# Opening stage of a two-layer perceiver kernel: load order, split of the queries, and idle products on TensorE

## What is computed

```python
x = x + _L0_xattn_ref(_layernorm(x, axis=-1), ctx_2048, ctx_2048)
# in it, with 16 heads of 16 channels, keys = values = ctx_2048:
scores = jnp.einsum('bhqd,bhkd->bhqk', qh, kh) / math.sqrt(hd)
qi = jnp.arange(Sq)[:, None] + (Sk - Sq)
ki = jnp.arange(Sk)[None, :]
causal = ki <= qi
scores = jnp.where(causal[None, None], scores, jnp.asarray(MASKED_BIAS, scores.dtype))
attn = jax.nn.softmax(scores, axis=-1)
out = jnp.einsum('bhqk,bhkd->bhqd', attn, vh)
```

## Time and profile before

| | us |
|---|---|
| three runs | 490.94, 493.5, 493.93 (median 493.5) |
| the profiled execution | 491.93, its span 490.1 |
| busy in the span: PE, DVE, ACT, POOL | 418.6, 334.4, 267.0, 110.0 |
| chain that ended last, shares | PE 63%, DVE 18%, ACT 7%, issue 6% |
| opening, up to the first product of scores | 24.94 |
| maxima of group 0, up to the copy of its maximum to rows | 24.94 to 37.91 |
| group 0 | 37.91 to 57.03 |
| group 1 | 57.03 to 73.50 |

### The profile page before, as it was taken

The page is one execution under the profiler, slowest core; times in us unless marked ns, Lnnn a source line. Parts: engine busy times, 40 slices in busy tenths (PEclk is TensorE's granted clock), DMA queues, the critical chain, the costliest instruction groups (busy, mean ns, idle before and its releaser), DMA issues.

```text
span 490.1 us, 9082 instructions
## 1 busy us (share of the span) xinstructions
PE 418.6 (85%) x3628; PEld 307.4 (63%) x3628; DVE 334.4 (68%) x537; ACT 267.0 (54%) x594; POOL 110.0 (22%) x88
## 2 busy tenths in 40 slices
PE   0168789998978898998998889996999799999997
PEld 0115556665645586486444624445889689999996
DVE  3788766678568977894366654865554788877872
ACT  4405887776758717431233315556771286777762
POOL 3002346001294010000022352233000203333300
PEclk9999999999989999999999979998899799999999
DMA  6599186543751078137200000019300595540000
GB/s 226 130 256 277 25 202 174 141 120 90 185 197 48 3 235 305 44 123 297 95 1 1 0 3 0 1 45 361 109 2 0 168 346 175 172 172 1 1 2 23
DMA packets 25002, 58.28 MB, mean 119 GB/s; under 512 B 5209, under 2 KB 13689, under 8 KB 21114
## 3 DMA queue, kind: packets, MB, share of 16 engines
q1 hardware_dynamic: 24960, 57.69, 37.2%
HBM read 44.77 MB, written 0.29 MB: 92 GB/s over the span
## 4 chain that ended last, share of the span: by engine, by line
PE 63%; DVE 18%; ACT 7%; issue 6%; POOL 2%; DMA 2%; SPq 0%; ACTq 0%; DVEq 0%; POOLq 0%
PE ps L1289 19%; PE ps L1093 9%; PE ps L924 7%; PE ps L911 5%; PE ps L880 4%; DVE mx L1666 3%; ACT reg_b L683 3%; PE ps L959 2%; PE ps L1254 2%; PE ps L1244 2%; PE ps L1243 2%; PE ps L1003 2%; POOL qreg L472 2%; PE ps L1090 1%; DMA x<-in_x 1%
## 5 line engine op out<-in xcount | busy, mean ns | idle before, releaser
L1666 DVE TENSOR_REDUCE mx<-ps 128x1 f32<-128x1024 f32 x64 | 77.0, 1221 | 36.5 <-PE ps L880 24.9
L683 ACT ACTIVATE reg_b<-ps 128x512 f32<-128x512 f32 x128 | 74.9, 598 | 26.6 <-PE ps L911 17.2
L911 PE MATMUL ps<-qreg,reg_b 98*128 98x128 bf16 x512 | 47.3, 225 | 5.7 <-ACT reg_b L683 4.2
L1093 PE MATMUL ps<-reg_b,xT 128*128 128x512 f32 x96 | 49.8, 643 | 0.0
L1289 PE MATMUL ps<-part_a 128*128 128x256 f32 x384 | 48.2, 283 | 0.4 <-DVE part_a L1819 0.4
L911 PEld LDWEIGHTS ps<-qreg,reg_b 98*128 98x128 bf16 x512 | 35.2, 100 | 19.8 <-ACT reg_b L683 9.7
L1289 PEld LDWEIGHTS ps<-part_a 128*128 128x128 f32 x384 | 46.9, 192 | 0.6 <-DVE part_a L1819 0.6
L396 POOL TENSOR_TENSOR rstd<-ve,cf 128x1 f32<-128x1 f32 x12 | 6.8, 567 | 174.0 <-DVE ve L1362 174.0
L822 ACT ACTIVATE reg_a<-ps,b 128x256 f32<-128x256 f32 x64 | 30.2, 472 | 24.4 <-PE ps L1289 24.4
L924 PE MATMUL ps<-reg_b 128*32 128x128 f32 x1024 | 43.0, 285 | 0.3 <-ACT reg_b L683 0.3
L880 PE MATMUL ps<-reg_b,qreg 96*128 96x512 bf16 x96 | 34.3, 427 | 10.2 <-DMA reg_b<-reg_b 7.5
(11 more groups left out here) (279 smaller groups left out, 849.1 us busy)
## 6 DMA issues: line engine op xcount, KB each, us to landing
reg_b<-in_w SPq DMA_DIRECT2D x16, 512.0 KB, 7.6
reg_b<-in_w SPq DMA_DIRECT2D x8, 1024.0 KB, 7.3
reg_b<-reg_b SPq DMA_DIRECT2D x56, 128.0 KB, 3.2
reg_b<-in_w_qkv SPq DMA_DIRECT2D x3, 2048.0 KB, 7.5
reg_b<-reg_a SPq DMA_DIRECT2D x40, 128.0 KB, 3.2
reg_a<-in_ctxK SPq DMA_DIRECT2D x4, 1024.0 KB, 7.5
reg_a<-in_ctx SPq DMA_DIRECT2D x8, 512.0 KB, 4.7
reg_b<-bc_mem SPq DMA_DIRECT2D x4, 1024.0 KB, 6.6
```

The lines of the kernel that those rows point to most:

```text
L683: sc.activation(pT[n % 3], score_b[n % 2], ACT.Exp).then_inc(S("exp_done"), 1)
L911: mm = pe.matmul(cols, kS[g % 3][0:SROWS, c // 8, j, P * (c % 8):P * (c % 8 + 1)], qT[b][0:SROWS, HPG * hg + j, :], start=not last, stop=True)
L1093: mm = pe.matmul(bank(b, n % 2), xT[b][:, i, :], w_qkv[j][:, i, 512 * n:512 * (n + 1)], start=False, stop=i == KD - 1)
L1666: ve.reduce_max(mx[:, piece // 2, piece % 2:piece % 2 + 1], score_a[m % 2].rearrange("p i k -> p (i k)"), X_AXIS).then_inc(S("max_done"), 1)
```

## The change

SP loads `cf` and both halves of K before `cb` and x of batch 1, which now counts on `const_in`. `split_queries` is cut into `scale_queries`, `query_part1`, `query_residue`, `query_part2` and `query_part3`; for batch 0 all five stand before the first `key_residue`. For batch 1 they and the layer norm move between the maxima of groups 1 and 2, in six places, and its inverse root on POOL behind the values of group 1. TensorE turns batch 1's queries in groups 2 and 3 instead of 1 and 2, and ACT copies them there. TensorE gets 30 idle products behind the first `key_part3`, three behind each pair of group 0's maxima, 12 before `max_to_rows(0)` and six behind it.

```diff
             load(x[0][:, :], io["x"][0], "x_in")
+            load(cf[:, :], io["cf"], "x_in")
             load(ctxK[:, 0, 0:2, :], io["ctxK"][0][:, 0:2, :], "ctxK_in0")
-            load(x[1][:, :], io["x"][1], "x_in")
-            load(cf[:, :], io["cf"], "const_in")
+            load(ctxK[:, 0, 2:4, :], io["ctxK"][0][:, 2:4, :], "ctxK_in1")
             load(cb[:, :], io["cb"], "const_in")
-            load(ctxK[:, 0, 2:4, :], io["ctxK"][0][:, 2:4, :], "ctxK_in1")
+            load(x[1][:, :], io["x"][1], "const_in")
...
-            pool.wait_ge(S("const_in"), 32)
+            pool.wait_ge(S("x_in"), 32)
             inv_sqrt(0, 0)
-            inv_sqrt(0, 1)
...
+                if g == 1:
+                    inv_sqrt(0, 1)
...
-                      (1, 8): [(late_query_rows, 0)], (1, 14): [(late_query_rows, 1)], (2, 8): [(late_query_rows, 2)],
-                      (2, 13): [(late_query_rows, 3)], (3, 9): [(state_rates,)], (4, 1): [(weigh_masked, 0)], (4, 12): [(transposed_x, 1, 0)],
+                      (2, 8): [(late_query_rows, 0)], (2, 13): [(late_query_rows, 1)], (3, 8): [(late_query_rows, 2)],
+                      (3, 13): [(late_query_rows, 3)], (3, 9): [(state_rates,)], (4, 1): [(weigh_masked, 0)], (4, 12): [(transposed_x, 1, 0)],
...
-            read_before_rows = {2: ("qT_sb", 4), 3: ("qT_sb", 6), 5: ("z_sb", 1), 6: ("bc_copied", 1)}
+            read_before_rows = {3: ("qT_sb", 4), 4: ("qT_sb", 6), 5: ("z_sb", 1), 6: ("bc_copied", 1)}
...
+            pe.wait_ge(S("k3_done"), 1)
+            keep_busy(7, 30)
             for part in range(16):
                 scores_for_max(0, part)
+                if part % 2:
+                    keep_busy(7, 3)
+            keep_busy(7, 12)
             max_to_rows(0)
+            keep_busy(7, 6)
...
-            beside = {(0, 7): [(ln_stats, 0, 1)], (0, 8): [(ln_apply, 0, 1), (split_queries, 1)], (3, 8): [(masked_weight, 0)], (5, 2): [(weigh_outputs, 0)], (5, 3): [(normalise, 0)],
+            beside = {(1, 1): [(ln_stats, 0, 1)], (1, 3): [(ln_apply, 0, 1), (scale_queries, 1)], (1, 5): [(query_part1, 1)],
+                      (1, 6): [(query_residue, 1)], (2, 5): [(query_part2, 1)], (2, 6): [(query_part3, 1)], (3, 8): [(masked_weight, 0)], (5, 2): [(weigh_outputs, 0)], (5, 3): [(normalise, 0)],
...
+            scale_queries(0)
+            query_part1(0)
+            query_residue(0)
+            query_part2(0)
+            query_part3(0)
             key_residue(0)
-            split_queries(0)
             key_residue(1)
```

More of the change, by code:

```diff
@@ L1033, in misc_read @@
                 pe.wait_ge(S(name), count)
-            beside = {(1, 6): [(late_query_columns, 0)], (1, 11): [(late_query_columns, 1)], (2, 6): [(late_query_columns, 2)],
-                      (2, 11): [(late_query_columns, 3)], (4, 11): [(misc_read, "o_all", 4), (x_to_columns, 1, 0)], (4, 13): [(step_sizes, 0)],
+            beside = {(2, 6): [(late_query_columns, 0)], (2, 11): [(late_query_columns, 1)], (3, 6): [(late_query_columns, 2)],
+                      (3, 11): [(late_query_columns, 3)], (4, 11): [(misc_read, "o_all", 4), (x_to_columns, 1, 0)], (4, 13): [(step_sizes, 0)],
                       (5, 2): [(keep_busy, 6, 18)],
                       (5, 4): [(misc_read, "o_all", 5), (state_maps, 0)],}
-            read_before_rows = {2: ("qT_sb", 4), 3: ("qT_sb", 6), 5: ("z_sb", 1), 6: ("bc_copied", 1)}
+            read_before_rows = {3: ("qT_sb", 4), 4: ("qT_sb", 6), 5: ("z_sb", 1), 6: ("bc_copied", 1)}
             parts_at = {}
@@ L1359, in ln_stats @@
                     ve.wait_ge(S(f"x_done{b}"), t)
+                else:
+                    ve.wait_ge(S(("x_in", "const_in")[b]), 32)
                 link(ve.bn_stats(stats[b][:, :], x[b][:, :]))
@@ L1386, in key_part3, with scale_queries, query_part1, query_residue @@
                                  ks3[b][1][:, 2 * pair:2 * pair + 2, :], ALU.subtract).then_inc(S("k3_done"), 1)
-            def split_queries(b):
+            def scale_queries(b):
                 ve.wait_ge(S(f"xn_done{b}"), 1)
+                link(ve.tensor_scalar(tmp[b][:, :], xn[b][:, :], 1.0 / math.sqrt(HD0), None, ALU.mult))
+            def query_part1(b):
+                q = tmp[b][:, :].rearrange("p (h d) -> p h d", h=H0)
+                link(ve.tensor_copy(q_split[b][:, :, 0:3, :], q.unsqueeze(2).to_broadcast([P, H0, 3, HD0])))
+            def query_residue(b):
                 q = tmp[b][:, :].rearrange("p (h d) -> p h d", h=H0)
                 r = tmp2[b][:, :].rearrange("p (h d) -> p h d", h=H0)
-                link(ve.tensor_scalar(tmp[b][:, :], xn[b][:, :], 1.0 / math.sqrt(HD0), None, ALU.mult))
-                link(ve.tensor_copy(q_split[b][:, :, 0:3, :], q.unsqueeze(2).to_broadcast([P, H0, 3, HD0])))
                 link(ve.tensor_tensor(r, q, q_split[b][:, :, 0, :], ALU.subtract))
+            def query_part2(b):
+                r = tmp2[b][:, :].rearrange("p (h d) -> p h d", h=H0)
                 link(ve.tensor_copy(q_split[b][:, :, 3:5, :], r.unsqueeze(2).to_broadcast([P, H0, 2, HD0])))
+            def query_part3(b):
+                r = tmp2[b][:, :].rearrange("p (h d) -> p h d", h=H0)
                 ve.tensor_tensor(q_split[b][:, :, 5, :], r, q_split[b][:, :, 3, :], ALU.subtract)\
```

4 lines of the change are left out of this document (2 added, 2 removed).

## The result

| | before | changed |
|---|---|---|
| median of 11 runs each, us | 492.27 (490.94 to 493.93) | 488.94 (487.15 to 491.13) |
| ratio to before, 95% interval | | 0.9935 [0.9909, 0.9961] |
| profiled execution, its span | 491.93, 490.1 | 488.57, 486.8 |
| first product of scores | 24.94 | 22.66 |
| T, rows of group 0's maximum | 37.91 | 33.78 |

The changed kernel is 0.65% faster, 3.2 us, within the 1% that counts as no change here. Ratios use fast runs alone, and the one slow run that the argument uses is the profiled execution of the kernel without idle products, 499.12 us.

The account below looks back on a forecast made before the run. DVE was taken to bound the opening and group 0's maxima, with TensorE, ACT and DVE handing on in groups 0 and 1. Terms gave -3.3, the clock's fall +2.3: -1.0 from 492.7 to 491.7 us, range 489.0 to 494.6.

Parts of the forecast that it names:

- Opening, -2.5: Before the first scores: earlier `cf` lets DVE start the queries sooner, third parts end at 19.4, scores could start 22.45; -2.5 us.
- Idle products ahead, +0.3: Thirty idle products before the first scores, with the clock rising near 22, end at 22.8: +0.3 us, bounds 0 and 1.3.
- Maxima, -1.2: Group 0's maxima: faster first pair -0.4, statistics gone -0.65, faster transposes of `nm` -0.2, reductions stay 9.74; -1.2 us.
- Group 0, 18.4: Between group 0's and group 1's maximum rows: DVE becomes the bound, 18.4 us against 19.12; -0.7, bounds -1.5 and 0.
- The wait, about 4 us: TensorE idles about 4 us for group 1's maxima; the clock falls behind it, costing 2.3 us.
- Group 1, 19.3: Group 1 forecast at 19.3 us; two DVE instructions behind its sixth and seventh next reductions add 0.5; the clock term is 2.3.
- Group 3, +0.3: Two ACT copies of about 0.57 and eight transposes come into group 3: +0.3 us, bounds 0 and +1.2.
- Sum at group 4, -1.0: All terms up to group 4: -3.3 us without the clock, +2.3 for its fall, together -1.0.
- Rival (a): The clock holds through TensorE's wait for group 1's maxima: -3.3, 489.4 us, chance 0.22.
- Rival (b): The clock falls 6.8 us behind that wait and DVE-bound group 1 cannot catch up: +0.1, 492.8 us, chance 0.15.
- Rival (c): Slower: idle products run at half clock into group 0's maxima and TensorE bounds there: +3.8, 496.5 us, chance 0.07.
- Rival (d): In the opening `cf` lands late, DVE starts its queries where it did: +1.5, 494.2 us, chance 0.06.

Follow-up runs that it names:

- kernels but the last: Changed kernel with batch 1's side work as before, 18, 8 and 26 idle products in early waits, 30 and 22 in two late ones: 484.4 us, ratio 0.9838.

## Why the prediction was right, and where it was not

That the change stays within 1% of before held (0.65%, forecast with a chance of 0.90); the 491.7 were 2.8 us too high, and the range ended 0.06 us above the median of the changed kernel. The second ten runs of it, 490.41, lie inside. Part of this is the width of that class, about 4.9 us to each side: the sum said -1.0 us, and timed it is -3.2 and -2.5. By its steps, from the profile of the changed kernel, with the second execution of it behind a stroke:

- **Opening, -2.5: right, -2.3.** The third parts end at 19.57 where 19.4 was worked out, and both halves of the edit were shown to be needed. `xn` started 0.6 later than I took it to, at 5.99: I went by when POOL was free, but the statistics wait for `cf` too, which let them start at 4.42, and `xn` stands 1.57 behind their start, as it did before (6.80 and 8.37).
- **Idle products ahead, +0.3: 0 / 0.** They end at 22.21 and the copies land at 22.66. The clock rose sooner than the 22 us that I took: thirty products took 4.78, where thirty at half clock took 6.22 in the run with them alone. When it rises differs between executions. The second one of the changed kernel took 5.27, and the other kernels with the new opening took 4.86 to 5.96; the two longest, 5.78 and 5.96, held the scores back by 0.4 and 0.6.
- **Maxima, -1.2: mis-sized, -1.85.** From the first score to T it is 11.12 us, before 12.97. The step that failed is "the reductions stay: 9.74". They took 9.14: one lasts 1.21, as before, but the next starts sooner. It is the full clock that does this: 9.14 too in the run with the idle products alone, 9.74 in both runs without them. By these runs the full clock is worth 1.24 from the first score to T and the statistics, which left that stretch, 0.61.
- **T at 34.5: 33.78 / 33.86.** The 0.7 are 0.65 of the maxima and 0.3 of the idle products, less the 0.2 that the opening gave short.
- **Group 0, 18.4: 18.65 / 18.58.** The first reduction comes at T + 3.75 (3.6). The reading that DVE bounds the group was right, and 16.7 without the pieces is shown.
- **The wait, about 4 us: 3.80 / 3.81, and the clock fell**, as forecast. The Trainium skill (TensorE: Matmul & The Clock Gate, "Why this matters for your kernels") warns of such idle gaps, and here the trace agrees: with the wait filled the clock held and 3 us came back. My rows for it (held behind 2.13, fell behind 2.95 and 3.84) were one execution: behind the same 2.13 the clock fell in three of the four other kernels that have this wait.
- **Group 1, 19.3: 19.24 / 18.11.** The fall was longer in the one execution (6.8 us) and shorter in the other (3.4).
- **Group 2, no term: +1.23 / 0.** The fall at 71.20 behind 0.90 of idle time was not foreseen.
- **Group 3, +0.3: +0.5.** 14.94 against 14.43; with ACT's copies and the transposes back in groups 1 and 2 it is 14.43 again.
- **Sum at group 4, -1.0: -0.1 / -2.4.** My sum lies between the two.
- **"Everything after group 4 only moves along": wrong, or at least not shown.** From group 4 to the end the two executions of the changed kernel took 3.2 and 1.1 us less than the one of before, with unchanged work. The falls of the clock there come at the same waits but last 3.4 or 6.8 us, differently in each execution: 20.4 us in both, 23.8 in the one before. This is not of the change alone. From the rows of group 7's maximum to the end the work is the same in all kernels but the last, and it took from 327.4 to 332.0 us: 332.0 in the kernel before, 327.4 and 329.7 in the changed one, 327.4 to 331.7 in the others. One execution can thus be off by more than the whole effect. Whether the changed stage has any part in it stays open.

Rival (a) named nearly the measured time, 489.4, but by a mechanism that did not happen: the clock did not hold through the wait. Rival (b), a fall of 6.8 us, is what the profiled execution shows, and at group 4 it stands at -0.1 where (b) had +0.1; its end came out earlier by the part behind group 4. Rival (c) did not happen in the changed kernel; half of its mechanism, idle products that end late, showed when they stand behind the old opening, by 0.8 us, and by 0.4 and 0.6 in two executions behind the new one. Rival (d) did not happen.

What I did not see at all is the price of the move. I counted its pieces where they went, and never asked what the place that they left had cost: behind `nm` of group 0 DVE waits for TensorE anyway, 4.22 us of it in the changed kernel. Five steps of 4.4 us left an idle engine for a stretch in which the same engine is the bound. My own first reduction "3.6 after T" said so. Put back, the change is worth 6.9 us instead of about 3 (ratio 0.9859 [0.9807, 0.991], four runs).

The best of the runs are the four kernels with the new opening, the idle products and the early work, or most of it, behind `nm` of group 0, 484.4 to 485.6 us, ratios 0.9838 to 0.9862. Which of them is best can't be told.

## What to carry to other kernels

Price a move twice: what the work costs where it goes, and what stands idle where it was; work beside an idle stretch that another engine's start sets is nearly free, and the same work inside the engine's own chain costs its whole length. Idle products that raise the clock pay where they lie under a wait for data and end before it does. Leave them room: the same thirty took from 4.78 to 6.22 us from one execution to the next, whether they started at 17 or at 20, and the longest held the scores up by 0.8. And measure a filled wait by the time, not by the clock: here 11 us of half clock were mended with 1 us won that can't be told from nothing; where another engine or the loads set the end, a faster TensorE only waits longer. And size by repeated runs: one execution differed from the next by up to 4.6 us in work that was the same.

## What the runs showed of the hardware beyond that

- The same idle time had different ends. With 3.80 or 3.81 us idle ahead of group 1's maxima the clock fell in all five executions that have this wait, for 6.8 us in two and 3.4 in three. With 2.13 it held there in the kernel before and in the one with part of the work moved, and fell for 3.4 in three others. With 0.87 to 0.90 ahead of group 2's it fell in two executions and held in three. In the run with the idle products alone it read 0.53 over 7 us in which TensorE was busy for 6.53.
- A row of reductions of PSUM runs at 1.14 us from one to the next (9.14 for eight) with TensorE at full clock and at 1.22 (9.74 for eight) with it at half, with the same duration of one. It is so in all three kernels without idle products in group 0's maxima and in all with them.
- DVE and POOL took longer on work in SBUF when both were at it: DVE's subtraction of 128x256 took 2.08 instead of 0.51 beside POOL's subtractions, its cast 1.73 instead of 1.01, the last subtraction, beside POOL's copy, 1.44 instead of 1.02, POOL's four 9.36 instead of 8.38; a cast of 128x768 beside POOL's copy took 2.17 instead of 1.45. The kernel before has it too: `xn` and `tmp` of batch 1, beside POOL's copies from 37.25, took 1.27 and 1.01 instead of 0.41 and 0.28. A reduction that reads PSUM, beside the same subtractions, kept its 1.22.
